# One-hot rows with the token innermost and 16-bit operands, row numbers made by GpSimd

## The reference, cut

```python
def _route(tokens, router_w):
    capacity = int(math.ceil(T / E * CAPACITY_FACTOR))
    probs = jax.nn.softmax(tokens @ router_w.T, axis=-1)
    top1_idx, top1_prob = jnp.argmax(probs, axis=-1), jnp.max(probs, axis=-1)
    order = jnp.lexsort((-top1_prob, top1_idx))
    sorted_e = top1_idx[order]
    counts = jnp.bincount(top1_idx, length=E)
    start = jnp.cumsum(counts) - counts
    keep_sorted = jnp.arange(T) - start[sorted_e] < capacity
    keep = jnp.zeros((T,), bool).at[order].set(keep_sorted)
    return jnp.where(keep, top1_idx, 0)
...
x = x + xattn(layernorm(x), ctx, ...)
tokens = layernorm(x).reshape(T, D); final_e = _route(tokens, router_w)
for e in range(E):
    y = relu(tokens @ W1[e] + b1[e]) @ W2[e] + b2[e]
    out = out + jnp.where((final_e == e)[:, None], y, 0.0)
return x + out
```

## Time and profile before

| | us |
|---|---|
| median of 3 runs | 544.47 (543.80 to 544.93) |
| the profiled execution | 545.08 |
| its span | 543.3 |
| busy in the span: PE, PE's weight loads, DVE, ACT, POOL | 378.2, 307.1, 377.3, 353.1, 197.7 |

### The profile page before, as it was taken

One profiled execution on the slowest core, in us unless ns is written; L12 is line 12 of the kernel. 1 busy time (PEld: TensorE's weight loads), 2 busy tenths in 40 slices (PEclk: granted clock), 3 DMA queues, 4 the chain that ended last, 5 costly groups with the idle time before them and its releaser, 6 DMA issues.

```text
span 543.3 us, 10418 instructions
## 1 busy us (share of the span) xinstructions
PE 378.2 (70%) x2861; PEld 307.1 (57%) x2861; DVE 377.3 (69%) x941; ACT 353.1 (65%) x827; POOL 197.7 (36%) x276
## 2 busy tenths in 40 slices
PE   0370418999999889957876322233999999998940
PEld 0230005689999744426553222032999999998940
DVE  2999998478888869967898788796355555444520
ACT  1589987687878549949983443052677777776720
POOL 7300093244444300000000000003777777777774
PEclk9999999999999969978989555568799999999985
DMA  9920000000000000000336950002767666665511
GB/s 216 246 71 1 1 0 0 2 1 2 0 0 0 1 1 1 0 0 1 80 79 121 256 129 0 1 1 83 226 224 230 224 226 223 216 233 198 201 54 34
DMA packets 45137, 48.67 MB, mean 90 GB/s; under 512 B 10232, under 2 KB 32800, under 8 KB 45088
## 3 DMA queue, kind: packets, MB, share of 16 engines
q1 hardware_dynamic: 39728, 38.59, 24.0%
q0 software_dynamic: 4096, 8.46, 5.9%
q10 hardware_dynamic: 1264, 1.03, 0.7%
HBM read 16.20 MB, written 8.45 MB: 45 GB/s over the span
## 4 chain that ended last, share of the span: by engine, by line
PE 48%; DVE 23%; ACT 15%; DMA 5%; issue 4%; POOL 3%; SPq 0%; DVEq 0%; POOLq 0%; ACTq 0%
PE psum L1138 11%; PE psum L1147 10%; PE psum L956 6%; PE psum L972 5%; DVE big L1546 4%; PE psum L964 2%; ACT xqT L759 2%; POOL out L594 2%; DMA keys<-in_ctx 2%; ACT tok_b L759 2%; ACT big L662 2%; DMA out<-xall,src_of 2%; DVE xqT L1628 2%; DVE part L1322 2%; ACT big L619 1%
## 5 line engine op out<-in xcount | busy, mean ns | idle before, releaser
L587 POOL DMA_INDIRECT xall<-token_rows,src_of x64 | 61.7, 964 | 202.7 <-DVE slot_of L1675 183.5
L828 ACT ACTIVATE xqT<-psum,feat 128x128 f32<-128x128 f32 x284 | 81.0, 368 | 32.6 <-PE psum L1138 30.7
L1138 PE MATMUL psum<-xqT,feat 128*128 128x128 f32 x568 | 77.3, 281 | 0.0
L1147 PE MATMUL psum<-keys,xqT 128*128 x568 | 75.7, 277 | 0.3 <-issue 0.2
L1138 PEld LDWEIGHTS psum<-xqT,feat 128*128 128x128 f32 x568 | 71.4, 198 | 0.0
L594 POOL DMA_INDIRECT out<-xall,src_of x64 | 62.9, 983 | 19.5 <-issue 11.0
L1147 PEld LDWEIGHTS psum<-keys,xqT 128*128 128x128 f32 x568 | 68.9, 192 | 1.3 <-issue 0.9
L1703 DVE TENSOR_TENSOR xqT<-psum,feat 128x128 f32<-128x128 f32 x71 | 20.7, 292 | 52.2 <-PE psum L1147 51.7
L561 POOL TENSOR_TENSOR qb<-qb,arec 128x308 f32<-128x308 f32 x32 | 21.8, 699 | 64.6 <-DVE arec L1380 64.6
L972 PE MATMUL psum<-probT,keys 78*128 78x128 f32 x256 | 35.3, 285 | 1.8 <-ACT probT L724 1.8
L1697 DVE TENSOR_SCALAR xqT<-xall 128x128 f32 x71 | 25.8, 363 | 12.1 <-DMA xall<-token_rows,src_of 11.1
(11 more groups left out here) (301 smaller groups left out, 933.9 us busy)
## 6 DMA issues: line engine op xcount, KB each, us to landing
feat<-keys SPq DMA_DIRECT2D x71, 322.0 KB
token_rows<-xall SPq DMA_DIRECT2D x4, 1040.0 KB, 8.1
xall<-in_x SPq DMA_DIRECT2D x8, 512.0 KB, 7.3
keys<-in_L_ffn_W SPq DMA_DIRECT2D x1, 2048.0 KB, 13.2
keys<-in_L_ffn_W SPq DMA_DIRECT2D x8, 256.0 KB, 7.5
keys<-in_ctx SPq DMA_DIRECT2D x4, 462.0 KB, 6.8
xall<-token_rows,src_of POOLq DMA_INDIRECT x64
out<-xall,src_of POOLq DMA_INDIRECT x64, 2.3
```

The lines of the kernel that those rows point to most:

```text
L587: pool.indirect_dma_start(xring[:, t % RING, :], None, rows, bass.IndirectOffsetOnAxis(ap=src_of[:, t:t + 1], axis=0)).then_inc(s_g[t % TU ...
L828: m = act.activation(hT[a % DEPTH][:, P * c:P * c + P], bank(2 + a % 2)[:, P * c:P * c + P], ACT.Relu, bias=w_now[a % AHEAD][:, FF + c:FF ...
L1138: m = pe.matmul(bank(2 + a % 2)[:, P * c:P * c + P], w_now[a % AHEAD][:, P * c:P * c + P], gT[a % DEPTH], start=True, stop=True)
L1147: m = pe.matmul(bank(4 + a % 2, E), hT[a % DEPTH][:, P * c:P * c + P], w2s[:, bass.ds(e, 1), c, :].rearrange("p e d -> p (e d)"), start=(c ...
```

## The change

The one-hot rows get another layout. Before, `hot_row` was (token column, row) with the 128 rows innermost; now each group's is (row, token column) with the 16 token columns innermost. So the comparison reads a table of row numbers that has each number 16 times in a row (128 x 16, `row_no_b`), and the rows of the tokens, `row_b`, as a run of 16 that is repeated 128 times. `row_b` is now bfloat16, where `t64_5` was float32. PE reads the weights of a token column with a step of 16 elements. The one-hot tiles are as they were, with a float32 operand.

The table no longer is a constant of 128 numbers made at the start. GpSimd makes it, 2,048 numbers in the upper half of `tok_b`, after its part in the attention and once `s_hq` has its eighth signal. DVE waits for it ahead of the first one-hot (`s_rno`, "row_numbers_made"). The changed file is six lines longer at the end; what was L1628 is L1634, L1665 is L1671, L1112 is L1117.

```diff
-        row_no_b = sb("row_no_b", [P, P], BF16)
+        row_b = sb("row_b", [P, B], BF16)
...
-        hot_row = xqT[:, :].rearrange("p (t r) -> p t r", t=B)
+        hot_row = [xqT[:, i * HT * P:(i + 1) * HT * P].rearrange("p (r t) -> p r t", t=HT) for i in range(B // HT)]
+        row_no_b = tok_b[:, T // 2:T // 2 + P * HT].rearrange("p (r t) -> p r t", t=HT)
...
@@ block.gpsimd
-            pool.iota(row_no_b[:, :], pattern=[[1, P]], base=0, channel_multiplier=0,
-                      allow_small_or_imprecise_dtypes=True).then_inc(s_const, 1)
...
             attention_steps(lambda a, b, body: for_loop(pool, a, b, body), step)
+            pool.wait_ge(s_hq, HS)
+            pool.iota(row_no_b, pattern=[[1, P], [0, HT]], base=0, channel_multiplier=0,
+                      allow_small_or_imprecise_dtypes=True).then_inc(s_rno, 1)
...
@@ block.tensor, place(i)
-                    pe.matmul(bank(2, 2 * TILES), hot_row[:, t, :], hot_tile[:, t, :, :].rearrange("p a c -> p (a c)"),
+                    rows_of = hot_row[i][:, :, t % HT]
+                    pe.matmul(bank(2, 2 * TILES), rows_of, hot_tile[:, t, :, :].rearrange("p a c -> p (a c)"),
                               start=t == 0, stop=t == B - 1)
                     n = t % QUARTER
-                    m = pe.matmul(psum[:, 3, n * TILES:(n + 1) * TILES], hot_row[:, t, :], hot[:, t, :],
+                    m = pe.matmul(psum[:, 3, n * TILES:(n + 1) * TILES], rows_of, hot[:, t, :],
...
@@ block.vector
-            do(dve.scalar_tensor_tensor(t64[5][:, :], t64[4][:, :], -float(P), position, ALU.mult, ALU.add))
+            do(dve.scalar_tensor_tensor(row_b[:, :], t64[4][:, :], -float(P), position, ALU.mult, ALU.add))
+            dve.wait_ge(s_rno, 1)
...
-                dve.tensor_tensor(hot_row[:, t, :], row_no_b[:, :].unsqueeze(1).to_broadcast([P, HT, P]),
-                                  t64[5][:, t].unsqueeze(2).to_broadcast([P, HT, P]), ALU.is_equal).then_inc(s_hr, 1)
+                dve.tensor_tensor(hot_row[i], row_no_b, row_b[:, t].unsqueeze(1).to_broadcast([P, P, HT]),
+                                  ALU.is_equal).then_inc(s_hr, 1)
```

More of the change, by code:

```diff
@@ L364, in xattn_moe @@
         s_ps = sem("prefixes_ready")
+        s_rno = sem("row_numbers_made")
         s_ht = sem("one_hot_tiles_ready")
```

## The result

| | before | after |
|---|---|---|
| median of the device time | 544.88 us (14 runs) | 541.98 us (14 runs) |
| lowest and highest | 543.41 to 546.08 | 540.19 to 543.02 |
| ratio after / before, 95% interval | | 0.9949, 0.9937 to 0.9961 |
| profiled execution: time, span | 545.08, 543.3 us | 541.29, 539.5 us |

The change makes the kernel 2.8 us faster (2.1 to 3.4 by the interval). The forecast was 4.2 us faster; the measured time is inside the range, 1.7 us above the forecast of 540.3. The largest step came true: the row one-hots take what was predicted. Two terms are missing from the saving, one of about 1 us at 286 us and one of a quarter of a microsecond at the weights.

A forecast was written before the change was run, and what follows sets the result against it. DVE's unbroken chain from the one-hots to src_of, on which the gathers hang, was taken as the bound. DVE -4.24 us, the rest 0 to +0.05, made 544.47 - 4.2 = 540.3 us, range 538.9 to 543.0.

The forecast's parts named there:

- The four row one-hots: DVE's row comparisons before the gathers: 1.14 us a piece in place of 2.20, together 4.24 us saved.
- ACT becomes the pace: In the one-hot stage ACT, needing 2.37 us a group, sets the pace; PE ends 0.29 us ahead of DVE.
- The weights: PE's loads of columns now 32 bytes apart: 100 ns a pair, 0.22 us in the last group, covered.
- the dearest bound: Upper end for PE's stepped loads, two at float32 pace, 222 ns a pair; rival at 547.1 us, chance 0.09.
- The row numbers: GpSimd's iota of 2,048 numbers from 286.1 us: 1.8 us long, ending near 288, costing the path nothing.
- The bound of 0.8 us: Most that the iota could cost one DVE instruction at 286 to 288 us, from L1344's 1.51 against 0.75 us.
- my signs of being wrong: Listed: L1634 at 2.2 us, pairs 148 ns apart or more, DVE twice as long at 286 to 288, longer slow clock.
- The sum: Whole kernel: DVE -4.24 us, the rest 0 to +0.05, so -4.2 us from 544.47 to 540.3 us.
- the predicted 370.2: Time in us at which GpSimd's first gather was to come, against 374.38 before.
- The clock at the start of the loop: PE's half clock from 380 to 386 us might not move with the pause: 1 us either way allowed, zero taken.
- a late clock: Rival: PE's clock rises late in the loop, giving back one to two microseconds, 541.5 to 542.3 us; chance 0.05.

The follow-up runs named there:

- blocks of four or two: After, with one-hots of 4 or 2 token columns side by side, columns 8 or 4 bytes apart: ratio 1.0002 and 1.0143 against before.
- the kernel with float32 row numbers: After, with the iota moved into the threshold search and row_b as float32: 544.53 us against 544.46 for before, ratio 1.0004.

## Why the prediction was right, and where it was not

**The four row one-hots: right.** 1.14 us a piece was predicted and measured. With dense enough weights the place stage becomes 17.87 - 13.60 = 4.27 us shorter, against 4.24.

**ACT becomes the pace: nearly.** It works without a pause, and its groups start 2.28 us apart and not 2.37, as fast as DVE delivers.

**The weights: right in size, wrong in how.** A pair measured 124 ns at full clock; I had taken 100. By my working 124 ns is 15 x 39 = 0.59 us in the last group, of which 0.29 is covered: +0.3, and the traces show 13.87 - 13.60 = 0.27. But it isn't the last group alone. I held each group against ACT's 2.37 us and put the point from which PE falls behind at 148 ns, at full clock. At half clock a pair takes 160 ns, dense or not, and 16 of them 2.56 us, more than the 2.28 in which the next group is there. So PE starts full-clock work with a backlog and then, at 124 ns, gains on it only 0.3 us a group. How long half clock lasts counts with these weights: in the four profiles of this layout with fast one-hots the pairs change pace 4.27, 4.61, 4.93 and 5.08 us after the first, and the place stage takes 13.87, 13.94, 14.04 and 14.09. That 0.27 is what my working gives is therefore partly chance; by the other three profiles it is 0.34 to 0.49. With blocks of four or two the change comes after 2.98, 3.93, 3.93, 4.73 and 5.21 us, as scattered and once later than in any of the four, and the place stage takes 13.59 to 13.61 in all five: at 85 to 90 ns PE is through with its backlog before DVE asks. So it is the 124 ns that lets a long half clock reach DVE. When the clock rises differs from execution to execution in the other kernels too; the kernel with float32 row numbers still has 160 ns in its second group, up to 5.23 us, although PE has pauses there. What sets that moment wasn't tried and stays open. As to the two rules of the Trainium skill: "SBUF — State Buffer" (the note on cachelines) would make columns 32 bytes apart dear and those 4 bytes apart cheap, and the sign is as measured, 124 and 85 ns; the 124 is far from the 222 of the dearest bound, so that "TensorE: Matmul & The Clock Gate" (Weight-path perf modes), by which a strided read keeps the fast load, isn't refuted either.

**The row numbers: the step that failed.** "I take nothing, since the large tensor_scalar of this place, L1464, is what the iota waits for and is over." Two things in it were wrong. The price of an iota was taken per element, from tables of 64 and 128 numbers in one run each; with runs of sixteen the 2,048 cost 2.47 us and not 1.8. And I looked for a large instruction that could be disturbed, where a small one is enough: L1207 has 16 elements and waits for the whole rest of the iota, with DVE's queue behind it. The bound of 0.8 us was drawn from a meeting in which DVE lost part of its own length; the loss is what is left of GpSimd's instruction, whatever DVE's length. That fits as well: 86.27 - 85.31 = 0.96 us of the fill were left when L1344 began, and it ended 0.55 us behind the fill. In after the path is 1.1 us longer than in an undisturbed execution, 0.3 beyond my bound. Slower instructions at 286 to 288 us stood among my signs of being wrong, and that sign came. The Trainium skill has this rule, in "SBUF — State Buffer" (Who interferes with whom): whichever of the two engines starts first holds the shared ports for its whole instruction, and of DVE's instructions tensor_scalar is among those that ask for them, tensor_tensor against a GpSimd instruction that only writes is not, and neither is the form of tensor_scalar that also writes out its accumulator. The first two agree with the traces: L1207 was held for what was left of the iota (1.51 us), L1201 kept its 0.18 us. The third isn't tested here: L1551 in the search kept its 0.74 us, but it also reads PSUM. Read against DVE's queue at 286 us, this rule would have given the term.

**The sum.** With both terms it is -4.0 + 1.1 = -2.9 us, and -2.8 (-3.4 to -2.1) was measured, two thirds of the 4.2 forecast. The other 0.4 of the 1.7 us above the forecast is the start of my sum: 544.47 was the median of three runs of before, and it is 544.88 over 14. That the first gather came at 370.55, near the predicted 370.2, is partly chance: up to 283 us the profiled execution of after was 0.56 us ahead of that of before.

**The clock at the start of the loop: wrong.** I allowed a microsecond either way and gave a late clock a chance of 0.05. With the clock at 1.00 throughout the stretch nothing moved. The earlier trace rows shows PE busy 4.83 of 6 us at half clock, and I read that as PE being late; what it didn't show was who waited for PE. In the same row GpSimd is busy 4.47 of 6 us, all but its 0.30 us between issues.

## What to carry to other kernels

An instruction moved to an idle engine isn't free because the engine is idle: go through what the other engines have queued during its whole run, however small. If one of those is of the kind that stood still here (a tensor_scalar from SBUF to SBUF beside an iota), price the move at its full length or put it where no such instruction is queued. A table for a comparison can often be short and repeated by a step of zero outside, with a run of two inside: that keeps two elements at a time, keeps the columns close together and makes the table cheap. And before a slow clock is given a price, find the engine that issues without gaps in that stretch; if it isn't TensorE, the clock is worth nothing there as long as TensorE has time in hand.

## What the runs showed of the hardware

- GpSimd's iota is priced by the lengths of its runs as much as by its elements: 128 numbers in one run 0.24 us, 256 in runs of two 1.52, 2,048 in runs of sixteen, four and two 2.47, 4.42 and 11.35 us.
- A tensor_scalar from SBUF to SBUF on DVE that starts beside an iota does its work when the iota has ended: 16 elements took 1.51, 3.46 and 10.40 us in place of 0.16, and ended 0.03 to 0.04 us after the iota. The reverse order shows too: an iota of one column, 0.14 us, took 0.64 behind such a tensor_scalar. The PSUM-reading instructions of the search ran beside the same iota at their usual 0.74 us, and a tensor_tensor of 16 elements at its 0.18.
- Pairs of bf16 weight loads of 128 columns with 128 and 64 columns sent behind: 85 ns with columns next to each other, 85 with 4 bytes, 90 with 8 and 124 with 32 bytes between their starts, all at full clock; 160 ns at half clock with any of these steps.
- tensor_tensor takes bf16 two at a time (1,218 ns for 2,048 elements) with a run of sixteen and with a run of two repeated outside by a step of zero; with one float32 operand, or with the one value repeated in the innermost dimension, it takes 2,286 ns.
- An indirect DMA of this kernel holds GpSimd for 0.97 us and then 0.30 to the next, 1.28 us each, and 128 of them, one after another, fill 163.4 of the 168.9 us of this kernel's last stage.
